# Projecting queries and keys of two groups in five stages of seven block products instead of two stages and direct key products per group

## The reference, cut to what matters

```python
x = x + attn(cond(x, L0_cond_weights, itok), wq, wk, wv, wo)    # cond: per batch a 32x32 matrix picked by itok
x = x + ffn(cond(x, L0_cond2_weights, itok), qweight, weight_scale, bias)

def attn(x, wq, wk, wv, wo):        # H = 32 query heads, KV = 8 key and value heads, HD = 128
    q = rope(x @ wq);  k = rope(x @ wk);  v = x @ wv
    scores = (q @ k.T) / sqrt(128)   # four query heads share one key head: a group
    att = softmax(causal(scores))    # 32 x 32 for each batch and head
    return (att @ v) @ wo            # 4096 -> 512

def ffn(x, qweight, weight_scale, bias):    # FP8 rounding of x and of the result, by the largest value of each
    ...
```

## Time and profile before

| | us |
|---|---|
| median of 3 runs | 521.12 (521.07 to 521.58) |
| the profiled execution, its own time | 521.22 |
| span of its trace | 519.3 |
| PE busy | 501.1 (96%) |
| DVE busy | 418.6 (81%) |
| POOL busy | 310.2 (60%) |
| ACT busy | 248.2 (48%) |

### The profile page before, as it was taken

One profiled execution on the slowest core, in us unless ns is written; L12 is line 12 of the kernel. 1 busy time (PEld: TensorE's weight loads), 2 busy tenths in 40 slices (PEclk: granted clock), 3 DMA queues, 4 the chain that ended last, 5 costly groups with the idle time before them and its releaser, 6 DMA issues.

```text
span 519.3 us, 9226 instructions
## 1 busy us (share of the span) xinstructions
PE 501.1 (96%) x3148; PEld 401.5 (77%) x3150; DVE 418.6 (81%) x662; ACT 248.2 (48%) x475; POOL 310.2 (60%) x308
## 2 busy tenths in 40 slices
PE   8999999999999999999999999999999999999990
PEld 6888888877888888888888888888888887788530
DVE  5468967899688877978797879787978798985896
ACT  2652644564446453735472637263726354232523
POOL 0668688888669746884788388838874754200000
PEclk9999999999999999999999999999999999999996
DMA  7346111320502050104010410131300014000004
GB/s 263 140 145 204 41 62 62 101 82 1 163 1 62 1 162 1 59 3 158 10 51 13 149 33 27 39 122 57 104 1 21 1 43 168 0 2 1 0 0 162
DMA packets 32644, 35.27 MB, mean 68 GB/s; under 512 B 2251, under 2 KB 22859, under 8 KB 32620
## 3 DMA queue, kind: packets, MB, share of 16 engines
q1 hardware_dynamic: 32620, 34.96, 21.1%
HBM read 28.66 MB, written 6.29 MB: 67 GB/s over the span
## 4 chain that ended last, share of the span: by engine, by line
PE 89%; DVE 4%; POOL 3%; issue 1%; DMA 1%; ACT 0%; DVEq 0%; ACTq 0%; SPq 0%; POOLq 0%
PE bank L733 23%; PE bank L734 22%; PE bank L735 22%; PE bank L803 3%; PE bank L792 3%; PE bank L705 3%; PE bank L706 3%; PE bank L707 3%; PE bank L676 1%; POOL q_rot L392 1%; PE bank L861 1%; PE bank L938 1%; POOL wq_lo L378 1%; PE bank L687 1%; DVE xacc L1324 1%
## 5 line engine op out<-in xcount | busy, mean ns | idle before, releaser
L392 POOL TENSOR_TENSOR q_rot<-q_rot,q_swap 128x512 f32<-128x512 f32 x64 | 88.2, 1377 | 60.9 <-DVE q_swap L1070 60.9
L521 ACT ACTIVATE q_swap<-bank 64x512 f32<-64x512 f32 x80 | 47.7, 596 | 124.3 <-PE bank L735 76.9
L733 PE MATMUL bank<-wo_hi,o_hi 128*128 128x512 f32 x256 | 101.4, 396 | 0.8 <-issue 0.6
L734 PE MATMUL bank<-wo_lo,o_hi 128*128 128x512 f32 x256 | 99.8, 390 | 0.0
L735 PE MATMUL bank<-wo_hi,o_lo 128*128 128x512 f32 x256 | 99.7, 390 | 0.0
L1118 DVE TENSOR_TENSOR xacc<-xacc,bank 128x512 f32<-128x512 f32 x64 | 43.7, 683 | 35.8 <-PE bank L735 35.7
L1070 DVE TENSOR_TENSOR q_swap<-q_swap,cst 128x512 f32<-128x512 f32 x80 | 60.2, 752 | 0.0
L733 PEld LDWEIGHTS bank<-wo_hi,o_hi 128*128 128x128 f32 x256 | 48.1, 188 | 13.1 <-issue 2.6
L735 PEld LDWEIGHTS bank<-wo_hi,o_lo 128*128 128x128 f32 x256 | 48.1, 188 | 10.2
L734 PEld LDWEIGHTS bank<-wo_lo,o_hi 128*128 128x128 f32 x256 | 48.1, 188 | 9.5
L387 POOL TENSOR_TENSOR wo_lo<-raw_o,wo_hi 128x512 fp32r<-128x512 f32 x32 | 45.5, 1444 | 9.5 <-ACT wo_hi L507 9.5
(11 more groups left out here) (160 smaller groups left out, 1042.3 us busy)
## 6 DMA issues: line engine op xcount, KB each, us to landing
raw_q<-in_L_attn_wq SPq DMA_DIRECT2D x16, 512.0 KB, 4.0
raw_o<-in_L_attn_wo SPq DMA_DIRECT2D x8, 1024.0 KB, 7.0
v_st<-values SPq DMA_DIRECT2D x16, 256.0 KB, 4.4
xacc<-in_x SPq DMA_DIRECT2D x4, 512.0 KB, 7.5
raw_k<-in_L_attn_wk SPq DMA_DIRECT2D x8, 256.0 KB, 4.3
out<-xacc SPq DMA_DIRECT2D x8, 256.0 KB, 2.0
values<-v_more SPq DMA_DIRECT2D x6, 256.0 KB, 2.1
raw_o<-in_L_attn_wv SPq DMA_DIRECT2D x1, 1024.0 KB, 8.1
```

Source lines behind the costliest of these rows:

```text
L392: pool.tensor_tensor(item_out(h, k), item_out(h, k), q_swap[(h + k) % 2][:], ALU.add).then_inc(rope_done, 1)
L521: act.activation(dst[0:P // 2, :], ps[P // 2:P, :], ACT.Copy)
L733: pe.matmul(dst, l_hi, r_hi, start=(i == 0), stop=False)
L734: pe.matmul(dst, l_hi, r_lo, start=False, stop=False)
```

## The change

Two groups now make a round p (0 to 3) of five stages i, and every stage is one pair of heads with seven block products. Stage 0 pairs the key head of group 2p with query head 0, stage 1 has query heads 1 and 2, stage 2 pairs query head 3 with the key head of group 2p+1, stages 3 and 4 have the four query heads of that group. `key`, `k_high`, `k_low` and their tiles and semaphores go. Four items a stage are roped instead of five. Product 0 now goes to the bank that the key had, which is also the bank of the second scores. Stages 0, 2, 3 and 4 of a round attend a unit each, stage 1 none. The output tiles are spread with `ahead` (before the attention), `behind` (after the products) and `end` (after the scores). Scores of group 2p are at the end of stage 2, of group 2p+1 at the end of stage 4. `raw_q` has a third slot. Both programs have the same opening up to the ninth value tile and the same tail.

```diff
-        product_ps = [one_ps, b_ps, c_ps, d_ps, b_ps, c_ps, e_ps]
-        item_ps = [k_ps, d_ps, b_ps, c_ps, e_ps]
+        product_ps = [a_ps, b_ps, c_ps, d_ps, b_ps, c_ps, e_ps]
+        item_ps = [d_ps, b_ps, c_ps, e_ps]
...
-V_BEFORE = (9, 11, 15, 16)
+V_BEFORE = (9, 11, 13, 15, 16)
```

GpSimd, the order within a stage, and what it splits in which stage:

```diff
+            def stage(p, i, split_wo=None):
+                more = not is_last(p, i)
                 if more:
-                    sum_weights(*follow)
...
-                if split_wo is not None:
-                    wo_low(split_wo, 0, wo_lo)
-                    wo_low(split_wo, 1, wo_lo)
-                rope_add(g, h, 0)
-                if split_wo is not None:
-                    wo_low(split_wo, 2, wo_lo)
-                    wo_low(split_wo, 3, wo_lo)
+                    sum_weights(*following(p, i))
+                if split_wo is not None:
+                    for head in range(REP):
+                        wo_low(split_wo, head, wo_lo)
                 if more:
-                    for i in range(4):
-                        q_low(*follow, i)
-                for k in range(1, 5):
-                    rope_add(g, h, k)
+                    for m in range(4):
+                        q_low(*following(p, i), m)
+                for k in range(ITEMS):
+                    rope_add(p, i, k)
                 if more:
-                    if h == 1:
-                        k_low(g + 1)
...
+                    for m in range(4, PRODUCTS):
+                        q_low(*following(p, i), m)
...
+                stage(p, 0)
+                stage(p, 1)
+                stage(p, 2, split_wo=None if isinstance(p, int) and p == 0 else 2 * p - 1)
+                stage(p, 3)
+                stage(p, 4, split_wo=2 * p)
```

ScalarE: after `o_high` and `keep_first` of a stage come now all four `wo_high`, then the exponential and four `q_high`. TensorE:

```diff
+            def products_of(p, i, last):
...
+                    pe.wait_ge(first_kept, n)
+                    if i in (0, 3):
+                        pe.wait_ge(s_turned, 4 * p + (0 if i == 0 else 2))
+                product(n, 0)
+                if first:
                     pe.wait_ge(t_lo_done, 3)
                 elif last is None:
-                    pe.wait_ge(rope_cos, 5 * n)
-                product(g, h, 1)
+                    pe.wait_ge(rope_cos, ITEMS * n)
+                product(n, 1)
...
+            def stage(p, i, last=None, fill=(), ahead=(), behind=(), end=(), side=None):
+                n = STAGES * p + i
+                for tile in ahead:
+                    project_out(*tile)
                 if last is not None:
-                    pe.wait_ge(rope_cos, 5 * n)
+                    pe.wait_ge(rope_cos, ITEMS * n)
+                    if i in (0, 3):
+                        pe.wait_ge(s_turned, 4 * p + (0 if i == 0 else 2) - 1)
                     attend(*last)
...
+                products_of(p, i, last)
+                for tile in fill:
+                    values(tile)
+                for tile in behind:
+                    project_out(*tile)
+                if side is not None:
+                    scores(p, side, 0)
+                    scores(p, side, 1)
+                for tile in end:
+                    project_out(*tile)
...
+            def stages(p):
+                stage(p, 0, last=(2 * p - 2, 1), ahead=tiles(2 * p - 2, 0, 3), behind=tiles(2 * p - 2, 1, 0, 1))
+                stage(p, 1, behind=tiles(2 * p - 2, 1, 2, 3))
+                stage(p, 2, last=(2 * p - 1, 0), behind=tiles(2 * p - 1, 0, 0, 1, 2), side=0, end=tiles(2 * p - 1, 0, 3))
+                stage(p, 3, last=(2 * p - 1, 1), behind=tiles(2 * p - 1, 1, 0, 1, 2))
+                stage(p, 4, last=(2 * p, 0), ahead=tiles(2 * p - 1, 1, 3), behind=tiles(2 * p, 0, 0, 1, 2), side=1)
+
+            stage(0, 0, fill=late[0])
+            stage(0, 1, fill=late[1])
+            stage(0, 2, fill=late[2], side=0)
+            stage(0, 3, fill=late[3])
+            stage(0, 4, last=(0, 0), behind=tiles(0, 0, 0, 1, 2), side=1)
```

VectorE, the same list with the softmax steps (`soft` takes the unit in `weights`, the steps in `steps`):

```diff
                 soft_part(0, 1, 2)
-                rope(g, h, 0)
+                for tile in ahead:
+                    accumulate(*tile)
...
+                rope(p, i, 2)
+                for tile in fill[0:1]:
+                    v_copy(tile)
+                for tile in behind[0:1]:
+                    accumulate(*tile)
+                rope(p, i, 3)
                 soft_part(5)
...
+                for tile in behind[1:2]:
+                    accumulate(*tile)
                 soft_part(6)
...
+                stage(p, 0, last=(2 * p - 2, 1), weights=(2 * p - 1, 0), steps=range(3), ahead=tiles(2 * p - 2, 0, 3),
+                      behind=tiles(2 * p - 2, 1, 0, 1))
+                stage(p, 1, weights=(2 * p - 1, 0), steps=range(3, SOFT_STEPS), behind=tiles(2 * p - 2, 1, 2, 3))
+                stage(p, 2, last=(2 * p - 1, 0), weights=(2 * p - 1, 1), behind=tiles(2 * p - 1, 0, 0, 1, 2), side=0,
+                      end=tiles(2 * p - 1, 0, 3))
...
+            stage(0, 3, weights=(0, 0), fill=late[3])
+            stage(0, 4, last=(0, 0), weights=(0, 1), behind=tiles(0, 0, 0, 1, 2), side=1)
```

489 lines of the change are left out of this document (219 added, 270 removed).

## The result

The changed kernel takes **553.6 us** (median of four runs, 550.6 to 554.9) against 521.35 for the kernel before: a ratio of **1.061**, interval 1.0566 to 1.0654. It is slower, as forecast, but by 32 us and not by 18, and above the range's 546. The profiled execution took 550.62, with a span of 548.8: 29.5 us longer than before. It is the shortest of the four runs, and the other three have no trace, so what follows accounts for 29.5 of the 32 us.

What follows compares the result with a forecast made beforehand. TensorE, busy 501.1 of 519.3 us, was taken as the bound, so its removed matmuls and new waits count in full. Terms summed to +18.2: span 537.5, plus 1.9 outside it, 539.4 us; range 530.5 to 546.

Steps and rivals of the forecast that it cites:

- 24 matmuls less, 6.7 us with half (1, 1): Over four rounds 24 matmuls go, -5.4 us; the loss in the old half (1, 1) goes too, -1.3.
- Opening +1.7: At the start product 1 waits for the third t_lo: +1.7 us, bounds 1.0 and 2.0.
- turn +0.8: Round 0, product 0 of stage 3 waits for both score transposes of stage 2: +0.8 us.
- stage (0, 4) +4.5: Round 0, stage 4's attention waits for softmax step 6, run behind stage 3's last rope: +4.5 us, bounds 4.0 and 5.0.
- Scores of stage (0, 2), +1.8: Round 0, stage 2's scores wait for all four rope_add, which end at +16.8 against 15.0 of matmuls: +1.8 us.
- Attention of stage 2, 3 x 2.5: Rounds 1 to 3, stage 2's attention waits for softmax step 6: 2.5 us each, +7.5, bounds 1.4 and 3.0 each.
- Scores of stages 2 and 4, 8.6 in sum: Scores wait for rope_add because GpSimd is late after wo_low, q_low and weight sums: +1.9 + 4.5 + 2.2 us.
- seven waits for rope_add that I named as a sign: Expected in TensorE's waits: rope_add before the scores, 1 to 2 us, seven times.
- Rival 3: The 4.5 us wait before stage (0, 4) also lowers TensorE's clock: 2.3 more, 541.7 us; chance 0.13 for above 542.
- the high bounds: All terms at their upper bounds, said to give 549 us with the clock.
- the 105.6 forecast: A round should take about 105.6 us where two groups took 102.0.
- the 108 from which I would have said that VectorE is the bound: Sign: rounds over 108 us mean VectorE has become the bound, its busy time near the round's length.

Runs made afterwards that it cites:

- light_hold: hold_full with GpSimd's wo_low in the loop cut to a quarter of its columns (part of the computation left out): 534.0 us, ratio 1.024.
- hold_full: Changed kernel with 14, 20 or 12 useless matmuls put into TensorE's five long waits: 553.6 us, ratio 1.061.
- three_tiles: Changed kernel with one output tile behind stage 0's products and three behind stage 1's: 555.8 us, ratio 1.065.
- three_wo: three_tiles and wo_order together, on the changed kernel: 543.1 us, ratio 1.040.
- best3: three_wo plus round 0 weight sums on VectorE, finer waits for freed banks, and useless matmuls before stage (0, 2)'s scores and stage (0, 4)'s attention: 539.1 us, ratio 1.035.
- wo_hold: wo_order and hold_full together, nothing left out: 538.4 us, ratio 1.032.
- wo_order: Changed kernel; in stages 2 and 4 ScalarE rounds two wo heads before the attended unit and GpSimd runs four rope_add before all q_low: 547.5 us, ratio 1.048.
- experiment 8: Three runs taking away both causes or only one: light_hold 534.0 us, wo_hold 538.4 us, three_light 540.8 us.
- three_light: three_tiles with GpSimd's wo_low in the loop cut to a quarter of its columns (part of the computation left out): 540.8 us, ratio 1.039.
- pause_34: Kernel before the change, TensorE paused at the end of each half of five loop groups for 3 or 4 dependent ScalarE copies: 567.0 us, ratio 1.086.

## Why the prediction was wrong, point by point

Two steps failed, and they overlap: the price and the place of GpSimd's lateness in stages 2 and 4, and the bound from which a wait costs clock. The other terms held or were missed by under 2 us.

- **24 matmuls less, 6.7 us with half (1, 1).** Held, as far as the sum shows it: light_hold comes out at 521.1 - 6.7 + 19.6 of waits.
- **Opening +1.7, turn +0.8, stage (0, 4) +4.5.** Measured 1.2, 0.9 and 4.8. Right, mechanism and size, within the bounds given.
- **Scores of stage (0, 2), +1.8.** Measured 3.5. The term was mis-sized: I took the tail from half (0, 1) of before, where GpSimd had idle time. Here the last rope_add ended at 95.9 us, 18.4 after product 0 (77.52), where half (0, 1) had 16.8. ScalarE's rows, after and then before, show where it begins:

```profile
84.55 0.73 ACT L508 ACTIVATE wq_hi<-w_sum 128x256 fp32r<-128x256 f32 x2 [4.57 <-POOL w_sum L404]
...
85.61 0.60 ACT L528 ACTIVATE q_swap<-bank 64x512 f32<-64x512 f32 x1
```

```profile
73.01 0.60 ACT L521 ACTIVATE q_swap<-bank 64x512 f32<-64x512 f32 x1 [0.26 <-DVE bank L1050]
```

  The first swap stands in ScalarE's list behind the rounding of weight sums, for which it waits 4.57 us, because GpSimd makes them behind the last rope_add of the stage before. So the swap starts 8.1 us after product 0 where it started 6.4 after it: 1.7 us, all that was missed. I had this cause for stage 1 of the later rounds, at 0.2, and not here. No run takes it away, so this is read from the rows and not tested.
- **Attention of stage 2, 3 x 2.5.** Measured 3.0, 3.0 and 3.2, at and just above my upper bound. Right mechanism, the size short by 1.7 in three rounds. GpSimd's weight sums hold back the first swap here too: in stage (2, 1) it starts 7.2 us after product 0.
- **Scores of stages 2 and 4, 8.6 in sum.** A step that failed. GpSimd was late for the reason given, but TensorE met the lateness elsewhere: not at the scores but one step earlier, at the third tile, since VectorE's accumulate of the first stands behind rope 2. I followed the chain rope_add to scores and not what else is queued behind it on VectorE. Of the seven waits for rope_add that I named as a sign one came, that of stage (0, 2). The 5.0 us seen in the trace are also not its price: with the long waits filled the same lateness costs 19.6 (hold_full 553.6 against light_hold 534.0), 3.4 of it two falls of the clock behind tile waits.
- **Rival 3, the other step that failed.** I had the mechanism, and let it decide "from a pause of about 3.5 us on; the waits of 2.5 stay below". That number was read from one place, the end of the program, where nothing came after the pause. Pauses of 2.28 already lower the clock in three of five cases, and the loss goes on when work is resumed. So it happened five times in the changed kernel and not once: 11.3 us for the 2.3 given. The Trainium skill, on TensorE: Matmul & The Clock Gate (Part 1: The HAM clock gate), has the idle array at half rate until it has been busy for a while; by that rule the second half of the loss was to be had in the prediction, and the trace agrees (0.50 at 180 to 182 us, with TensorE fully busy).
- **The sum itself.** I added places as if each wait were its own. They are not: one chain of GpSimd feeds the attention's softmax chain, the ropes and the tiles, so what goes at one place comes back at the next (three_tiles, hold_full, three_wo, best3). The range has a slip besides: the high bounds make 548.7 without the clock, not with it, and 551 with it. The measured 553.6 is above that too.

The way from the forecast to the measurement, by kernels (the second row changes two things, the width of wo_low and the order):

| from | to | us | what |
|---|---|---|---|
| 530.8, forecast without the scores' 8.6 | 534.0 light_hold | +3.2 | stage (0, 2) +1.7, attentions +1.8, the rest -0.3 |
| 534.0 | 538.4 wo_hold | +4.4 | GpSimd's full wo_low, in the better order |
| 538.4 | 547.5 wo_order | +9.1 | the clock |
| 547.5 | 553.6 changed kernel | +6.1 | the order: four q_low ahead of the ropes, all wo_high behind the rounding |

The forecast had 8.6 and no likely clock for the last three rows, which are 19.6. The split depends on the way taken: by hold_full it is 19.6 for GpSimd and nothing for the clock. The changed kernel, hold_full, wo_order and wo_hold are the four ways of taking away each cause, both or none: the clock gives 0 with GpSimd late and 9.1 without, the order 6.1 with the falls and 15.2 without them. The sum of the two is shown, and that they overlap.

The other outcomes that the prediction named: a round takes 108.3 us (178.51 to 286.84), above the 105.6 forecast and just above the 108 from which I would have said that VectorE is the bound. It is not: it is busy 89.5 of 109 us, and experiment 8 excludes it. A round's length alone was no sign for a cause. The windows of the changed kernel:

```profile
263.46:300.76 37.30, 34.43 (x173) 28.15 (x172) 31.69 (x50) 20.93 (x42) 32.34 (x35) 0.95 0.12 35
...
232.00:341.00 109.00, 103.80 (x663) 83.98 (x662) 89.54 (x141) 54.69 (x110) 81.09 (x85) 0.98 0.17 53
```

What the totals hide is in the first row: between the first rope_add of stage 0 and that of stage 2 GpSimd is busy for 32.3 of 37.3 us, 87%, while over the round it is at 74%.

## What to carry to other kernels

A wait of the busiest engine is not a term that can be added or taken away by itself: follow the chain behind it to the engine that is late, and ask at which place it shows next; then take that lateness away first. In a kernel like this one a wait of TensorE of 2.3 us or more is likely to cost 1.7 to 3.4 us of half clock beside its length (45 of 54 here), and waits under 2 us cost their length alone. Before instructions are moved into the gaps of an engine, see what runs on the other engines in these gaps.

## What the runs showed of the hardware

- TensorE's clock fell behind 3 of 5 pauses of 2.28 us and behind none of 1.62; one of 3.48 in three_light had no fall. A fall lost 1.7 or 3.4 us, and 5.1 in four kernels at the scores of stage (0, 2), where a second wait of 0.9 follows; it goes on after work is resumed. With 12 to 20 matmuls of no use in the wait it did not fall.
- Falls make the time of a kernel uneven: pause_34 spread by 5.5 us over four runs, with the granted clock, where light_hold, which has no falls in its rounds, spread by 0.6.
- GpSimd's q_low of 128x256 took 1.19 us beside VectorE's multiply of two SBUF tiles and 0.74 alone, the multiply 1.09 and 0.68: interleaving them costs both.
